# One buffer moved from the gate/up products to the w_down loads in a Mamba block with a ternary feed-forward

## The chip, the cores and the metric

The kernel runs on the 8 cores of one Trainium2 chip. The 4 x 4096 tokens are split into 8 runs of 2048 tokens, one for each core, and the cores do not exchange data. The time is that of the slowest core in device microseconds, from launch to end. Engines are called PE (TensorE, matrix products), DVE (VectorE), ACT (ScalarE), POOL (GpSimd) and SP (SyncE, which here only issues transfers).

## The reference

```python
xn = _layernorm(x, axis=-1)
x = x + _L0_attn_ref(xn, ...) + _L0_ffn_ref(xn, w_gate, w_up, w_down)

# _L0_attn_ref: a Mamba block (input projection, causal convolution, selective scan
# in chunks of 256 tokens, gating, output projection); the change does not touch it

def _weight_quant(w):                       # ternary weights, one scale for the matrix
    scale = 1.0 / jnp.clip(jnp.mean(jnp.abs(w)), 1e-05)
    return jnp.clip(jnp.round(w * scale), -1.0, 1.0) / scale
def _act_quant(x):                          # 8-bit activations, one scale for each token
    scale = 127.0 / jnp.clip(jnp.max(jnp.abs(x), axis=-1, keepdims=True), 1e-05)
    return jnp.clip(jnp.round(x * scale), -128.0, 127.0) / scale
def _bitlinear(x, w):
    return jnp.einsum('bsi,oi->bso', _act_quant(x), _weight_quant(w))
gate = silu(_bitlinear(x, w_gate))          # HIDDEN 1024 -> INNER 4096
up = _bitlinear(x, w_up)
return _bitlinear(gate * up, w_down)        # INNER 4096 -> HIDDEN 1024
```

## The kernel before

The program has four stages: normalization and weight casts, the Mamba block (which takes most of the time), the gate/up stage, and the down projection. A barrier stands between them. The change lies in the gate/up stage.

Every operation is recorded by a helper, `P.op`, with its queue (engine) and with the names (tags) of what it reads and writes. From the tags the helper derives the semaphore waits. An engine works through its list in the order in which the operations were recorded, and so does SP's queue: a transfer whose wait is not over holds all that were recorded behind it. Tags stand for buffers: a tile with two buffers has two tags, and a write to one of them waits only for the readers of that one.

The gate/up stage runs in eight passes, f = 0 to 7, of 512 of the 4096 inner columns each. For each pass:

- `f1_mm(f)` goes over the 16 tiles of 128 tokens (mt). For each it records 8 matmuls into a gate PSUM tile and 8 into an up PSUM tile (L939, 512 columns each; three such pairs of PSUM tiles take turns), then on ACT silu of the gate into `gsb` (L946) and the scaled up part into `usb` (L949), then on DVE the product of the two into `gu_bf` (L952) and its largest absolute value (L956). `gsb` and `usb` have two buffers each, by mt % 2.
- `f1_quant(f + 1)` makes the ternary weights of the next pass: 16 groups, 8 for gate and 8 for up, each a load of a 128 x 512 float32 tile on SP's queue into `wqf` (L916, two buffers) and two operations on DVE (L919 into `wts`, L923 into `wgq` or `wuq`). The weights of pass 0 are made before the passes start.
- `f1_wd` makes the ternary w_down for the next stage, in 64 pieces over all passes: a load of a 128 x 512 float32 tile on SP's queue into `wqf3` (L982, one buffer), two operations on DVE as one step (L986 into `wts`, L989 into `wdstg`, one buffer), and a store from `wdstg` to `s_wdq` on POOL's queue (L994).

`_sec(f)` mixes the last two: three steps of `f1_quant` (one whole group), then two steps of `f1_wd` (so that a load, a pair and a store fall on alternate places), and so on; at most 32 steps of `f1_wd` are taken in a pass, so that its 192 steps are used up in passes 0 to 5. `_zipf` records two steps of `f1_mm` for one step of `_sec`. The 48 + 32 steps of `_sec` thus lie beside the first 8 of the 16 token tiles of passes 0 to 5; the other 8 tiles have nothing beside them. Pass 6 has the 48 weight steps alone, and pass 7 nothing.

The trace names tiles by their allocation without the buffer's number, so that `wqf3` appears as `wqf` in it; its loads are told by their source, `wqf<-wdT`. The PSUM tiles appear as psB, psG (gate) and psC, psU (up).

Of the kernel before, what the change touches and what calls it, by code (L numbers as in the profile page):

```python
# [8 lines left out]
F32 = mybir.dt.float32  # L9
BF16 = mybir.dt.bfloat16  # L10
# [132 lines left out]
def build_program(TOK):  # L143
# [34 lines left out]
    def salloc(stack, name, shape, dt):  # L178
        return stack.enter_context(nc.sbuf_tensor(name, shape, dt))
# [5 lines left out]
    swbc = salloc(pstack, "swbc", [128, 9], F32)  # L185
# [60 lines left out]
         reads=["alraw"], writes=["alneg_t"])  # L246
    P.op("vector", lambda v: v.tensor_scalar_mul(alneg[:], alneg[:], -1.0),
         reads=["alneg_t"], writes=["alneg"])
# [4 lines left out]
        writes=["wcf:0"], dma=True)  # L253
    P.op("vector", lambda v: v.tensor_copy(wxT_bf[:], wcf[0][:, 0:16 * 96]),
         reads=["wcf:0"], writes=["wxT_bf"])
    P.op("sync", lambda e: e.dma_start(wcf[1][0:64, 0:DI], w_dtT.ap()),
         writes=["wcf:1"], dma=True)
    P.op("vector", lambda v: v.tensor_copy(wdtT_bf[:], wcf[1][0:64, 0:DI]),
         reads=["wcf:1"], writes=["wdtT_bf"])
# [569 lines left out]
    for sc in range(NSC):  # L829
# [7 lines left out]
        else:  # L837
# [11 lines left out]
         reads=["ones1"] + ["acc:%d:%d" % (wi2, t2) for wi2 in range(3)  # L849
                            for t2 in range(32)],  # L850
         writes=["psA"], wr_override=["psA"])
    P.op("scalar", lambda s: s.activation(acc[0:1, 0:96], psA[0:1, 0:96], AF.Copy,
                                          bias=0.0, scale=1.0),
         reads=["psA"], writes=["accr"])
    for wi in range(3):
        P.op("vector", lambda v, wi=wi: v.reduce_sum(
            swrow[0:1, 12 + wi:13 + wi], acc[0:1, wi * 32:(wi + 1) * 32], axis=AXX),
            reads=["accr"], writes=["swsum"])
    P.op("vector", lambda v: v.tensor_scalar(swrow[0:1, 0:3], swrow[0:1, 12:15],
                                             1.0 / NW_ELEMS, 1e-5, ALU.mult, ALU.max),  # L860
         reads=["swsum"], writes=["swclip"])
    P.op("vector", lambda v: v.tensor_scalar_mul(swrow[0:1, 3:6], swrow[0:1, 0:3], 0.5),
         reads=["swclip"], writes=["swthr"])
    P.op("vector", lambda v: v.tensor_scalar_mul(swrow[0:1, 6:9], swrow[0:1, 0:3], -0.5),
         reads=["swclip"], writes=["swnthr"])
    P.op("tensor", lambda t: t.matmul(psA[:, 0:9], ones2[0:1, 0:128], swrow[0:1, 0:9],
                                      start=True, stop=True),
         reads=["ones2", "swclip", "swthr", "swnthr"], writes=["psA"], wr_override=["psA"])
    P.op("vector", lambda v: v.tensor_copy(swbc[:], psA[:, 0:9]),
         reads=["psA"], writes=["swbc"])  # L870
# [6 lines left out]
    fstk = ExitStack()  # L877
# [3 lines left out]
    wqf = [salloc(fstk, "wqf%d" % i, [128, 512], F32) for i in range(2)]  # L881
    wts_1 = salloc(fstk, "wts", [128, 512], F32)
    wts = [wts_1, wts_1]
    gsb = [salloc(fstk, "gsb%d" % i, [128, 512], BF16) for i in range(2)]
    usb = [salloc(fstk, "usb%d" % i, [128, 512], BF16) for i in range(2)]
    wdstg = salloc(fstk, "wdstg", [128, 512], BF16)
    wqf3_1 = salloc(fstk, "wqf3", [128, 512], F32)
    wqf3 = [wqf3_1, wqf3_1]
    psG2 = fstk.enter_context(nc.psum_tensor("psG2", [128, 512], F32))
    psU2 = fstk.enter_context(nc.psum_tensor("psU2", [128, 512], F32))  # L890
    psG3 = fstk.enter_context(nc.psum_tensor("psG3", [128, 512], F32))
# [4 lines left out]
    for k2 in range(8):  # L896
        P.op("sync", lambda e, k2=k2: e.dma_start(
            xqfm[:, k2 * TOK:(k2 + 1) * TOK], s_xqfm.ap()[k2 * 128:(k2 + 1) * 128, :]),
            reads=["sxq:%d:%d" % (k2, i2) for i2 in range(NT)],
            writes=["xqfm:%d" % k2], dma=True)  # L900

    for i in range(NT):
        P.op("vector", lambda v, i=i: v.tensor_mul(
            combog[:, i:i + 1], invsx[:, i:i + 1], swbc[:, 0:1]),
            reads=["invsx:%d" % i, "swbc"], writes=["cg:%d" % i])
        P.op("vector", lambda v, i=i: v.tensor_mul(
            combou[:, i:i + 1], invsx[:, i:i + 1], swbc[:, 1:2]),
            reads=["invsx:%d" % i, "swbc"], writes=["cu:%d" % i])
# [20 lines left out]
    def f1_mm(f):  # L929
        fb = f % 2  # L930
        for mt in range(NT):
            gb = mt % 2
            psg, psgt = psGpool[mt % 3]
            psu, psut = psUpool[mt % 3]
            for (wtag, ps_, pst_) in (("wgq", psg, psgt), ("wuq", psu, psut)):
                wq_ = wgq[fb] if wtag == "wgq" else wuq[fb]
                for k2 in range(8):
                    yield lambda wq_=wq_, k2=k2, mt=mt, ps_=ps_, pst_=pst_, wtag=wtag, fb=fb: P.op(
                        "tensor", lambda t: t.matmul(  # L939
                            ps_[:, 0:512],  # L940
                            xqfm[:, k2 * TOK + mt * 128:k2 * TOK + (mt + 1) * 128],
                            wq_[:, k2 * 512:(k2 + 1) * 512], start=(k2 == 0), stop=(k2 == 7)),
                        reads=["xqfm:%d" % k2, "%s:%d:%d" % (wtag, fb, k2)],
                        writes=([pst_] if k2 == 0 else ()),
                        wr_override=([pst_] if k2 == 7 else ()))
            yield lambda gb=gb, mt=mt, psg=psg, psgt=psgt: P.op("scalar", lambda s: s.activation(  # L946
                gsb[gb][:], psg[:, 0:512], AF.Silu, bias=0.0, scale=combog[:, mt:mt + 1]),
                reads=[psgt, "cg:%d" % mt], writes=["gsb:%d" % gb])
            yield lambda gb=gb, mt=mt, psu=psu, psut=psut: P.op("scalar", lambda s: s.activation(  # L949
                usb[gb][:], psu[:, 0:512], AF.Copy, bias=0.0, scale=combou[:, mt:mt + 1]),  # L950
                reads=[psut, "cu:%d" % mt], writes=["usb:%d" % gb])
            yield lambda gb=gb, mt=mt, f=f: P.op("vector", lambda v: v.tensor_mul(  # L952
                gu_bf[:, mt * INNER + f * 512:mt * INNER + (f + 1) * 512],
                gsb[gb][:], usb[gb][:]),
                reads=["gsb:%d" % gb, "usb:%d" % gb], writes=["gu:%d:%d" % (mt, f)])
            yield lambda gb=gb, mt=mt, f=f: P.op("vector", lambda v: v.reduce_max(  # L956
                gmparts[:, mt * 8 + f:mt * 8 + f + 1],
                gu_bf[:, mt * INNER + f * 512:mt * INNER + (f + 1) * 512],
                axis=AXX, apply_absolute_value=True),
                reads=["gu:%d:%d" % (mt, f)], writes=["gmp:%d:%d" % (mt, f)])  # L960
# [17 lines left out]
    def f1_wd():  # L978
        for t in range(32):
            for hcol in range(2):  # L980
                wb9 = (t * 2 + hcol) % 2
                yield lambda t=t, hcol=hcol, wb9=wb9: P.op("sync", lambda e: e.dma_start(  # L982
                    wqf3[wb9][:], wdT.ap()[t * 128:(t + 1) * 128, hcol * 512:(hcol + 1) * 512]),
                    writes=["wqf3"], dma=True)
                def _wdq_pair(wb9=wb9):
                    P.op("vector", lambda v: v.tensor_single_scalar(  # L986
                        wts[0][:], wqf3[wb9][:], swbc[:, 8:9], ALU.is_le),
                        reads=["wqf3", "swbc"], writes=["wts"])
                    P.op("vector", lambda v: v.scalar_tensor_tensor(  # L989
                        wdstg[:], wqf3[wb9][:], swbc[:, 5:6], wts[0][:], ALU.is_ge,  # L990
                        ALU.subtract),
                        reads=["wqf3", "wts", "swbc"], writes=["wdstg"])
                yield _wdq_pair
                yield lambda t=t, hcol=hcol: P.op("gpsimd", lambda e: e.dma_start(  # L994
                    s_wdq.ap()[t * 128:(t + 1) * 128, hcol * 512:(hcol + 1) * 512],
                    wdstg[:]),
                    reads=["wdstg"], writes=["swdq:%d:%d" % (t, hcol)], dma=True)

    wd_it = iter(f1_wd())

    def _sec(f):
# [22 lines left out]
    for f in range(8):  # L1024
        _zipf(iter(f1_mm(f)), _sec(f), 2, 1)
# [3 lines left out]
    for mt in range(NT):  # L1029
        P.op("vector", lambda v, mt=mt: v.reduce_max(  # L1030
            sgu[:, mt:mt + 1], gmparts[:, mt * 8:mt * 8 + 8], axis=AXX),
            reads=["gmp:%d:%d" % (mt, f2) for f2 in range(8)], writes=["gmax:%d" % mt])
        P.op("vector", lambda v, mt=mt: v.tensor_single_scalar(
            invsgu[:, mt:mt + 1], sgu[:, mt:mt + 1], 1e-5, ALU.max),
            reads=["gmax:%d" % mt], writes=["gclip:%d" % mt])
        P.op("vector", lambda v, mt=mt: v.reciprocal(
            gmparts[:, mt * 8:mt * 8 + 1], invsgu[:, mt:mt + 1]),
            reads=["gclip:%d" % mt], writes=["grcp:%d" % mt])
        P.op("vector", lambda v, mt=mt: v.tensor_scalar_mul(
            sgu[:, mt:mt + 1], gmparts[:, mt * 8:mt * 8 + 1], 127.0),  # L1040
            reads=["grcp:%d" % mt], writes=["sgu:%d" % mt])
        P.op("vector", lambda v, mt=mt: v.tensor_scalar_mul(
            invsgu[:, mt:mt + 1], invsgu[:, mt:mt + 1], 1.0 / 127.0),
            reads=["gclip:%d" % mt], writes=["invsgu:%d" % mt])
        P.op("vector", lambda v, mt=mt: v.tensor_mul(
            combod[:, mt:mt + 1], invsgu[:, mt:mt + 1], swbc[:, 2:3]),
            reads=["invsgu:%d" % mt, "swbc"], writes=["cd:%d" % mt])
# [129 lines left out]
def _get_nc(TOK):  # L1177
    if TOK not in _NC_CACHE:
        _NC_CACHE[TOK] = build_program(TOK)
    return _NC_CACHE[TOK]  # L1180
# [62 lines left out]
```

How the kernel before makes its waits and increments, by code:

```python
                def body(eng, lst=lst, q=q):  # L119
                    sat = {}
                    last_inc = {}
                    for o in lst:
                        wl = {}
                        for d in o.waits:
                            if d.cum > wl.get(d.skey, 0):
                                wl[d.skey] = d.cum
                        for k in sorted(wl, key=lambda t: (t[0], t[1])):
                            v = wl[k]
                            if v > sat.get(k, 0):
                                eng.wait_ge(sems[k], v)
                                sat[k] = v
                        inst = o.fn(eng) if o.fn is not None else None
                        if o.inc:
                            k = o.skey
                            amt = o.cum - last_inc.get(k, 0)
                            inst.then_inc(sems[k], amt)
                            last_inc[k] = o.cum
```

## Time and profile before

| what | value |
|---|---|
| time, median of 2 runs | 5199.21 us (5197.51 to 5200.91) |
| time of the profiled execution | 5203.91 us |
| its span on the slowest core (core 0) | 5202.3 us (other cores 5163.9 to 5197.3) |
| busy: DVE, ACT, PE, POOL | 73%, 36%, 31%, 3% of the span |
| gate/up stage, first load issued to last product | about 4110 to 4748 us |

The profile shows one execution on the slowest core. An engine counts as busy while it executes; PE's share is that of pipelined matmuls and says little on how near it is to its peak. A line such as "L952" is that line of the kernel. In the waits a pair "A <- B" means that A stood idle until B was done. The stage that the change touches is one eighth of the span, and so the shares of the whole span say little about it; it is read by stretches.

### The profile page before, as it was taken

How to read it: one execution, taken by the hardware profiler on the slowest of the kernel's cores; microseconds unless marked ns; L12 is line 12 of the kernel's file. 1: busy time of each engine (PE TensorE's matmuls, PEld its weight loads, DVE VectorE, ACT ScalarE, POOL GpSimd, SP SyncE). 2: the span in 40 equal slices, each digit the busy share in tenths (PEclk: the TensorE clock that was granted, in tenths of full speed). 3: DMA queues.
4: the chain of work that ended last, by engine and by line, in shares of the span. 5: the costliest groups of instructions: out<-in, count | busy, mean ns of one | idle time of the engine just before them, and what ended most of it. 6: DMA issues, size and time to landing. Idle time of an engine off the chain costs nothing.

```text
span 5202.3 us, 47037 instructions; the slowest of 8 cores (5163.9 to 5202.3 us)
## 1 busy us (share of the span) xinstructions
PE 1622.3 (31%) x7308; PEld 818.5 (16%) x7308; DVE 3800.4 (73%) x10735; ACT 1858.8 (36%) x4106; POOL 151.6 (3%) x252
## 2 busy tenths in 40 slices
PE   0134111410321051033105103310200278776776
PEld 0122000200210030012002001200000033333332
DVE  3436888888888888888888888888888566653232
ACT  1335344434443434344333432433223022223342
POOL 0200000000000000000000000000000000000000
PEclk9996555755655575565557555655555689898998
DMA  7542002401410240041004002100100333321665
GB/s 239 170 116 69 0 21 72 122 0 47 135 33 0 89 126 0 25 129 53 0 0 118 1 0 61 57 0 0 49 0 0 110 118 102 101 90 37 205 219 190
DMA packets 311056, 378.41 MB, mean 73 GB/s; under 512 B 15522, under 2 KB 253218, under 8 KB 308644
## 3 DMA queue, kind: packets, MB, share of 16 engines
q1 hardware_dynamic: 282532, 266.34, 17.0%
q0 software_dynamic: 26496, 96.48, 5.3%
q10 hardware_dynamic: 1728, 12.58, 0.8%
q14 instruction: 234, 1.92, 0.1%
q8 instruction: 66, 1.08, 0.1%
HBM read 329.22 MB, written 46.14 MB: 72 GB/s over the span
## 4 chain that ended last, share of the span: by engine, by line
DVE 38%; issue 19%; PE 16%; DMA 14%; ACT 11%; DVEq 1%; SPq 0%; ACTq 0%; POOL 0%; POOLq 0%
DVE hbuf L677 12%; DVE dbub L670 6%; DVE ypb L699 4%; ACT dAb L661 4%; DVE ypb L695 3%; DMA wdqt<-s_wdq 3%; PE psBC L640 2%; PE psI L510 2%; PE psP L1119 2%; DVE yA L702 2%; PE psBC L647 2%; DMA wo_buf<-s_woutT 2%; DMA wch<-s_winT 2%; DVE pa L691 2%; DMA s_wdq<-wdstg 2%
## 5 line engine op out<-in xcount | busy, mean ns | idle before, releaser
L677 DVE TENSOR_TENSOR_SCAN hbuf<-dAb,dbub 128x256 bf16<-128x256 bf16 x2048 | 1398.5, 683 | 189.7 <-ACT dAb L661 189.4
L661 ACT ACTIVATE dAb<-delta_t,alneg 128x256 bf16<-128x256 bf16 x2048 | 906.0, 500 | 74.7 <-DVE hbuf L677 65.1
L640 PE MATMUL psBC<-shstB,ones 1*128 1x256 f32 x256 | 146.0, 669 | 2013.8 <-DVE shstB L637 2013.8
L651 ACT ACTIVATE Bsb<-psBC 128x256 bf16<-128x256 f32 x128 | 49.1, 383 | 1885.1 <-PE psBC L647 1845.0
L670 DVE TENSOR_TENSOR dbub<-du_t,Bsb 128x256 bf16<-128x256 bf16 x2048 | 579.6, 283 | 5.9 <-ACT Bsb L651 2.4
L702 DVE TENSOR_TENSOR yA<-yA,ypb 128x256 f32<-128x256 f32 x1024 | 435.1, 425 | 109.5 <-DVE ypb L699 4.5
L640 PEld LDWEIGHTS psBC<-shstB,ones 1*128 1x128 f32 x256 | 61.2, 295 | 2068.3 <-issue 2068.3
L699 DVE TENSOR_TENSOR ypb<-ypb,pa 128x256 bf16<-128x256 bf16 x896 | 261.7, 292 | 95.5 <-DVE ypb L695 3.2
L510 PE MATMUL psI<-xnsc,wch 128*128 128x256 bf16 x2048 | 307.2, 314 | 72.8 <-DMA wch<-s_winT 59.2
L752 PE MATMUL psOut<-wo_buf,gated 128*128 128x512 bf16 x256 | 118.5, 463 | 498.6 <-DVE gated L724 432.2
L695 DVE TENSOR_TENSOR ypb<-hbuf,Csb 128x256 bf16<-128x256 bf16 x1024 | 273.2, 267 | 0.0
L510 PEld LDWEIGHTS psI<-xnsc,wch 128*128 128x128 bf16 x2048 | 218.0, 112 | 166.5 <-issue 117.2
L691 DVE TENSOR_TENSOR pa<-hbuf,Csb 128x256 bf16<-128x256 bf16 x896 | 235.9, 263 | 0.0
L939 PE MATMUL psG<-wgq,xqfm 128*128 128x512 bf16 x640 | 171.3, 416 | 72.3 <-ACT gsb L946 71.9
L1119 PE MATMUL psP<-wdqt,guqT 128*128 128x512 bf16 x640 | 172.4, 409 | 46.1 <-DMA wdqt<-s_wdq 46.1
L939 PE MATMUL psU<-wuq,xqfm 128*128 128x512 bf16 x640 | 157.6, 391 | 0.0
L1079 DVE TENSOR_SCALAR tqg<-tqg 128x1024 int32<-128x1024 int32 x64 | 44.2, 691 | 149.7 <-ACT tqg L1073 149.2
L946 ACT ACTIVATE gsb<-psG,combog 128x512 bf16<-128x512 f32 x80 | 55.0, 688 | 226.5 <-DVE gu_bf L952 182.3
L1097 ACT ACTIVATE guqT<-psTf 128x1024 bf16<-128x1024 bf16 x64 | 65.4, 1022 | 186.1 <-PE psTf L1090 186.1
L919 DVE TENSOR_SCALAR wts<-wqf,swbc 128x512 f32<-128x512 f32 x128 | 62.0, 484 | 95.5 <-DMA wqf<-wuT 47.3
L647 PE MATMUL psBC<-shstC,ones 1*128 1x256 f32 x256 | 130.0, 607 | 0.0
L601 PE MATMUL psB<-dltbf,wdtT_bf 64*128 64x256 bf16 x128 | 48.0, 375 | 251.7 <-ACT xpb L605 231.5
(156 smaller groups left out, 3371.1 us busy)
## 6 DMA issues: line engine op xcount, KB each, us to landing
wch<-s_winT SPq DMA_DIRECT2D x128, 512.0 KB, 5.3
wdqt<-s_wdq SPq DMA_DIRECT2D x64, 1024.0 KB, 6.5
wo_buf<-s_woutT SPq DMA_DIRECT2D x64, 512.0 KB, 4.9
wab<-wgT POOLq DMA_DIRECT2D x32, 512.0 KB, 3.8
wab<-wuT POOLq DMA_DIRECT2D x32, 512.0 KB, 3.6
wab<-wdT POOLq DMA_DIRECT2D x32, 512.0 KB, 3.5
wqf<-wgT SPq DMA_DIRECT2D x64, 256.0 KB, 3.4
wqf<-wuT SPq DMA_DIRECT2D x64, 256.0 KB, 3.4
```

Of the source, the lines that this page charges most:

```text
L510: "tensor", lambda t: t.matmul(psI[mp][:, 0:CH], wch[wb][:, k2 * 256 + m * 128:k2 * 256 + (m + 1) * 128], xnsc[p][:, k2 * CH:(k2 + 1) * CH ...
L640: P.op("tensor", lambda t, bk=bk: t.matmul(psBC[bk][:, 0:CH], ones2[64:65, 0:128], shstB[64:65, :], start=True, stop=True), reads=["shB", ...
L647: P.op("tensor", lambda t, bk=bk: t.matmul(psBC[bk][:, CH:2 * CH], ones2[64:65, 0:128], shstC[64:65, :], start=True, stop=True), reads=["s ...
L661: P.op("scalar", lambda s, q=q, n=n, b=b: s.activation(dAb[b][:], delta_t[p][:, q * CH:(q + 1) * CH], AF.Exp, bias=0.0, scale=alneg[:, q * ...
L670: P.op("vector", lambda v, q=q, b3=b3, e2=e2: v.tensor_mul(dbub[b3][:], du_t[p][:, q * CH:(q + 1) * CH], Bsb[e2][:]), reads=["du:%d:%d" % ...
L677: P.op("vector", lambda v, b=b, b3=b3: v.tensor_tensor_scan(hbuf[b3][:], dAb[b][:], dbub[b3][:], 0.0, ALU.mult, ALU.add), reads=["dA:%d" % ...
L691: P.op("vector", lambda v, q=q, b3=b3, e2=e2: v.tensor_mul(pa[q][:], hbuf[b3][:], Csb[e2][:]), reads=["h:%d" % b3, "Csb:%d" % e2], writes= ...
L695: P.op("vector", lambda v, q=q, b=b, b3=b3, e2=e2: v.tensor_mul(ypb[b][:], hbuf[b3][:], Csb[e2][:]), reads=["h:%d" % b3, "Csb:%d" % e2], w ...
L699: P.op("vector", lambda v, q=q, b=b: v.tensor_add(ypb[b][:], ypb[b][:], pa[q][:]), reads=["yp:%d" % b, "pa:%d" % q], writes=["yp:%d" % b])
L702: P.op("vector", lambda v, q=q, b=b: v.tensor_add(yA[:, q * CH:(q + 1) * CH], yA[:, q * CH:(q + 1) * CH], ypb[b][:]), reads=["yA:%d" % q, ...
L939: "tensor", lambda t: t.matmul(ps_[:, 0:512], xqfm[:, k2 * TOK + mt * 128:k2 * TOK + (mt + 1) * 128], wq_[:, k2 * 512:(k2 + 1) * 512], sta ...
L1119: "tensor", lambda t: t.matmul(psP[pp][j][:, 0:512], guqT[gb][j][:, kb * 128:(kb + 1) * 128], wdqt[wb3][:, k3 * 512:(k3 + 1) * 512], start ...
```

## The change

`gsb` and `usb` go from two buffers each to one (128 x 512 bf16), and `wqf3` goes from one buffer to two (128 x 512 float32). The bytes that come free are those that are taken. The tags follow: one tag for `gsb`, one for `usb`, two for `wqf3`. No operation is added, removed or reordered.

```diff
-    gsb = [salloc(fstk, "gsb%d" % i, [128, 512], BF16) for i in range(2)]
-    usb = [salloc(fstk, "usb%d" % i, [128, 512], BF16) for i in range(2)]
+    gsb_1 = salloc(fstk, "gsb", [128, 512], BF16)
+    usb_1 = salloc(fstk, "usb", [128, 512], BF16)
+    gsb = [gsb_1, gsb_1]
+    usb = [usb_1, usb_1]
     wdstg = salloc(fstk, "wdstg", [128, 512], BF16)
-    wqf3_1 = salloc(fstk, "wqf3", [128, 512], F32)
-    wqf3 = [wqf3_1, wqf3_1]
+    wqf3 = [salloc(fstk, "wqf3_%d" % i, [128, 512], F32) for i in range(2)]
...
                 gsb[gb][:], psg[:, 0:512], AF.Silu, bias=0.0, scale=combog[:, mt:mt + 1]),
-                reads=[psgt, "cg:%d" % mt], writes=["gsb:%d" % gb])
+                reads=[psgt, "cg:%d" % mt], writes=["gsb"])
...
                 usb[gb][:], psu[:, 0:512], AF.Copy, bias=0.0, scale=combou[:, mt:mt + 1]),
-                reads=[psut, "cu:%d" % mt], writes=["usb:%d" % gb])
+                reads=[psut, "cu:%d" % mt], writes=["usb"])
...
                 gsb[gb][:], usb[gb][:]),
-                reads=["gsb:%d" % gb, "usb:%d" % gb], writes=["gu:%d:%d" % (mt, f)])
+                reads=["gsb", "usb"], writes=["gu:%d:%d" % (mt, f)])
...
                     wqf3[wb9][:], wdT.ap()[t * 128:(t + 1) * 128, hcol * 512:(hcol + 1) * 512]),
-                    writes=["wqf3"], dma=True)
+                    writes=["wqf3:%d" % wb9], dma=True)
...
-                        reads=["wqf3", "swbc"], writes=["wts"])
+                        reads=["wqf3:%d" % wb9, "swbc"], writes=["wts"])
...
-                        reads=["wqf3", "wts", "swbc"], writes=["wdstg"])
+                        reads=["wqf3:%d" % wb9, "wts", "swbc"], writes=["wdstg"])
```

## Rows read from the trace of the kernel before

**Rows 1.** Busy time by stretch (start:end length, engines, clock, DMA): first mixed half.

```profile
4154.58:4217.15 62.57, 45.99 (x181) 18.66 (x180) 41.40 (x71) 11.86 (x19) 5.41 (x10) 0.85 0.39 131
```

**Rows 2.** Waits, 4110 to 4760 us: who waited for whom: us, times, longest.

```profile
ACT gsb L946 <- DVE gu_bf L952: 288.8, 47, 9.7
...
DVE wts L919 <- DMA wqf<-wuT: 47.3, 30, 3.3
DVE wts L919 <- DMA wqf<-wgT: 42.8, 25, 7.0
...
DVE wts L986 <- DMA wqf<-wdT: 22.1, 30, 1.4
...
DVE wdstg L989 <- DMA s_wdq<-wdstg: 19.7, 29, 1.4
```

**Rows 3.** The 64 stores of L994: from issue to landing.

```profile
DMA to landing us min/median/max: 2.0/3.7/4.4
```

**Rows 4.** Timeline, two intervals: start us, us, engine, line, operation [idle before].

```profile
4163.78 0.75 DVE L989 SCALAR_TENSOR_TENSOR wdstg<-wqf,swbc,wts 128x512 bf16<-128x512 f32 x1
...
4165.07 0.55 POOL L994 DMA_DIRECT2D s_wdq<-wdstg  x1 [6.61 <-DVE wdstg L989]
...
4165.90 0.42 DVE L952 TENSOR_TENSOR gu_bf<-gsb,usb 128x512 bf16<-128x512 bf16 x1
...
4166.42 0.69 DVE L956 TENSOR_REDUCE gmparts<-gu_bf 128x1 f32<-128x512 bf16 x1
...
4167.31 0.49 DVE L986 TENSOR_SCALAR wts<-wqf,swbc 128x512 f32<-128x512 f32 x1 [0.20 <-DMA wqf<-wdT]
4168.59 0.75 DVE L989 SCALAR_TENSOR_TENSOR wdstg<-wqf,swbc,wts 128x512 bf16<-128x512 f32 x1 [0.80 <-DMA s_wdq<-wdstg]
4169.43 0.33 SPq L982 DMA_DIRECT2D wqf<-wdT  x1
...
4169.85 1.35 SPq L916 DMA_DIRECT2D wqf<-wgT  x2
...
4173.06 0.49 DVE L919 TENSOR_SCALAR wts<-wqf,swbc 128x512 f32<-128x512 f32 x1 [2.27 <-DMA wqf<-wgT]
...
4174.51 0.49 DVE L986 TENSOR_SCALAR wts<-wqf,swbc 128x512 f32<-128x512 f32 x1
4175.10 0.75 DVE L989 SCALAR_TENSOR_TENSOR wdstg<-wqf,swbc,wts 128x512 bf16<-128x512 f32 x1
```

**Rows 5.** L989 in passes 0 to 5: count, duration in ns, first and last start.

```profile
L989 DVE SCALAR_TENSOR_TENSOR wdstg<-wqf,swbc,wts x11: 750/752/752, 4156.6 to 4216.4; 128x512 bf16<-128x512 f32 x11
L989 DVE SCALAR_TENSOR_TENSOR wdstg<-wqf,swbc,wts x10: 750/752/752, 4235.6 to 4288.9; 128x512 bf16<-128x512 f32 x10
L989 DVE SCALAR_TENSOR_TENSOR wdstg<-wqf,swbc,wts x11: 750/752/752, 4310.5 to 4369.7; 128x512 bf16<-128x512 f32 x11
L989 DVE SCALAR_TENSOR_TENSOR wdstg<-wqf,swbc,wts x11: 750/751/752, 4391.2 to 4453.3; 128x512 bf16<-128x512 f32 x11
L989 DVE SCALAR_TENSOR_TENSOR wdstg<-wqf,swbc,wts x10: 750/751/752, 4473.2 to 4527.2; 128x512 bf16<-128x512 f32 x10
L989 DVE SCALAR_TENSOR_TENSOR wdstg<-wqf,swbc,wts x11: 750/752/753, 4548.8 to 4609.0; 128x512 bf16<-128x512 f32 x11
```

**Rows 6.** Timeline: PE's release at the first light half, then its pace there.

```profile
4213.89 0.69 ACT L946 ACTIVATE gsb<-psB,combog 128x512 bf16<-128x512 f32 x1 [5.50 <-DVE gu_bf L952]
...
4214.82 0.58 PE L939 MATMUL psB<-wgq,xqfm 128*128 128x512 bf16 x1 [3.15 <-ACT gsb L946]
...
4226.78 0.69 ACT L949 ACTIVATE usb<-psU,combou 128x512 bf16<-128x512 f32 x1 [0.98 <-PE psU L939]
4227.57 0.42 DVE L952 TENSOR_TENSOR gu_bf<-gsb,usb 128x512 bf16<-128x512 bf16 x1 [2.24 <-ACT usb L949]
...
4228.57 0.69 ACT L946 ACTIVATE gsb<-psB,combog 128x512 bf16<-128x512 f32 x1 [1.09 <-PE psB L939]
...
4231.03 0.42 DVE L952 TENSOR_TENSOR gu_bf<-gsb,usb 128x512 bf16<-128x512 bf16 x1 [2.24 <-ACT usb L949]
```

## The prediction

> **What bounds the kernel now.** I read the page first: the span is 5202.3 us, VectorE (DVE) is the busiest engine at 73%, and its 40 slices show that the end of the program is a different stage from the long scan. The change touches only tiles of the gate/up stage, so I looked for that stage's start and end by its lines (about 4110 to 4760 us) and then asked the trace for the waits in it, for single stretches of its timeline, and for the stretches it is made of.
>
> The stage is eight passes (f = 0 to 7). In passes 0 to 5 the first half is a *mixed half*: DVE quantizes the next pass's gate and up weights and, in between, w_down pieces. In the first mixed half PE is busy 46 of 62.6 us and DVE 41 [rows 1]: neither is full, so waits set the time. The waits of the whole stage name them [rows 2]: DVE waits 47.3 + 42.8 us for `wqf` loads, 22.1 us for `wqf3` loads (the trace calls them wqf<-wdT) and 19.7 us for the store that must leave `wdstg` before it is written again. ScalarE (ACT) waits 288.8 us for the product on DVE to free `gsb`. In the second half (the *light half*) DVE has only products and maxima to do and TensorE (PE) sets the pace.
>
> The unit to read is the interval from one w_down quantization (L989) to the next. By the order in which work is emitted there are two kinds: *short* ones with one weight group (L919 and L923) between two L989, and *long* ones with two. In passes 0 to 5 there are 58 intervals, 30 short and 28 long; 14 of the long ones also hold a product and its maximum. First to last L989 of the six passes adds up to 59.8 + 53.3 + 59.2 + 62.1 + 54.0 + 60.2 = 348.6 us [rows 5].
>
> A short one [rows 4]: L989 starts at 4163.78 and ends at 4164.53, POOL issues the store at 4165.07, and the next L989 starts at 4168.59 after a wait for that store. A long one follows: it ends at 4169.34, only then is the next `wqf3` load issued (4169.43), and queued behind it on SP's queue is a `wqf` load (4169.85). DVE stands for 2.27 us until that lands (4173.06), and L989 starts at 4175.10. The interval is 6.51 us.
>
> **wqf3, one buffer to two.** No instruction is added; 64 loads wait for the quantization two back instead of the last. In long intervals the removed wait is the one that sets the end: SP's queue is held by the `wqf3` load, not by the `wqf` buffer, so the second weight group's load can now leave as soon as the group two before it is done. That is before the previous L989 ends, one short interval earlier. With a load time of 3.2 us (4169.85 to 4173.06 [rows 4]) it has landed when DVE comes to it. What is late next? Two candidates:
>
> - the `wdstg` store, which the change leaves single: 0.54 us to its issue (4164.53 to 4165.07 [rows 4]), 3.7 us to landing (the median [rows 3]), 0.12 us to the next L989 (4165.07 + 3.4 landed, 4168.59 started), 0.75 us of L989: 5.11 us;
> - DVE's own work: a weight group costs 1.45 us (4173.06 to 4174.51 [rows 4]), the w_down pair, of the same two shapes, 1.45, product and maximum 1.2 (4165.90 to 4166.42 + 0.69). A long interval with a product is 3 x 1.45 + 1.2 = 5.55, without one 4.35, a short one 2 x 1.45 + 1.2 = 4.1 at most.
>
> So 30 short and 14 long intervals are set by the store at 5.11, and 14 by DVE at 5.55: 44 x 5.11 + 14 x 5.55 = 302.5. In short intervals the `wqf3` wait merely becomes a longer wait for the store. Saved: 348.6 - 302.5 = 46.1 us. Bounds: landings go from 2.0 to 4.4 us [rows 3]; I take the median because stores will still fly beside loads as now. Passes 6 and 7 hold no w_down work and save nothing.
>
> The Trainium skill (DMA: Bandwidth & Descriptors, Anatomy of one DMA) prices such a POOL-issued transfer at about 2.0 us plus its bytes over 436 GB/s, which for 128 KB is an estimated 2.3 us; by it the store would not bind at all and the sum would be that of the fast store below. The trace's 3.7 us median disagrees with it.
>
> **gsb and usb, two buffers to one.** Instructions and durations stay. `gsb` of token tile mt+1 now waits for the product of mt, not of mt-1. In the mixed half two products are some 5 us or more apart and gsb plus usb need 1.4, so DVE never waits for this. In the light half PE sets 3.46 us per tile (4227.57 to 4231.03 [rows 6]); usb ends at 4227.47, the product at 4227.99, and the next gsb starts at 4228.57 because PE's psB ends then. The new wait ends 0.5 us before the old one, so the pace stays. If that cover were gone it would cost at most its excess, tile by tile.
>
> What is lost is lead. In the mixed half PE runs until PSUM's three pairs and the two `gsb` are full, then stands: at 4214.82 it starts a tile after 3.15 us of standing, released by the gsb that the product just freed (4213.89 [rows 6]). With one buffer less, that same release lets it start the tile *before*: one more tile of 3.46 us is still to do in the light half, which ends with PE. This happens in every pass with a mixed half and in pass 6, whose first part has weight groups alone: 7 x 3.46 = 24.2 us more. Pass 7 is PE from end to end and adds none. Bounds: 0, if PE gets the tile done while DVE works off the other four, and 48 if each such tile ran at the lower of PE's two clock levels, 1.2 instead of 2.4 GHz, where it takes twice as long (the granted clock of 0.85 in [rows 1] shows both levels in a mixed half); 24.2 is nearest to the rows, since PE was standing at the release.
>
> **Sum.** 46.1 - 24.2 = 21.9 us less. The profiled execution (span 5202.3, time 5203.9) would become 5182; it lies 4.7 us above the median of the runs shown, 5199.2, so the forecast is 5199.2 - 21.9 = **5177 us**.
>
> **Rivals.**
>
> *Slow store (slower).* One mechanism: the `wqf3` and `wqf` loads leave earlier and lie over the store, which then lands later. At the longest landing seen, 4.4 us, the store interval is 0.54 + 4.4 + 0.12 + 0.75 = 5.81, above DVE's 5.55, so all 58 take it: 337.0, saved 11.6, lost 24.2: +12.6, **5212 us**. It decides from 348.6 - 58 x g = 24.2, g = 5.59, a landing of 4.18 us. For it: landings vary from 2.0 to 4.4 already. Against: today's stores leave in the same half microsecond as two loads [rows 4], and still take 3.7. The Trainium skill (SBUF — State Buffer, SBUF: two separate sides) says that DVE in some modes keeps POOL from writing descriptors, which speaks against packing DVE denser. The trace does not show it: at 4165.07 POOL issues on its usual 0.54 us while DVE has work.
>
> *Fast store.* With the loads spread out, stores land in 2.0 us (the shortest landing [rows 3]); then DVE alone sets the mixed half: 30 x 4.1 + 14 x 4.35 + 14 x 5.55 = 261.6, saved 87.0, less 24.2: **5136 us**. Against: many loads stay in flight.
>
> *The lost buffer is free.* PE fills its lead otherwise, and only the 46.1 counts: **5153 us**. Against: PE's stand at the release.
>
> *The change doesn't do what it says.* The long wait is written down to `wqf` loads, not `wqf3` [rows 2]; if `wqf`'s own buffers held them, long intervals would stay and only the 24.2 is left: **5223 us**. Against: SP issues that load 0.42 us behind the `wqf3` load [rows 4], while the group that frees its buffer was done before L989 began.
>
> **How the numbers follow.** Forecast 0.62 (its own range, landings of 3.4 to 4.0 us: store intervals 4.81 and 5.41, sums 289.3 and 315.7, so 5164 to 5191), slow store 0.14, lost buffer free 0.10, fast store 0.08, no effect on long intervals 0.06. The range from 5150 to 5210 holds the forecast, the free buffer and about half of the slow store; the two outer cases and the rest of the slow store stay out. Two per cent, about what a measurement of this kernel can tell from no change, is 104 us; no case lies further than 63 from the median. Hence 0.98 for within 2%, and 0.01 for each side for what I have not thought of.
>
> **What would show it.** Right: L986's waits for wqf<-wdT near 0; L919's waits for `wqf` down from 90 to about 30 us (the pass-0 weights ahead of the passes, and pass 6, keep theirs); L989's waits for the store up from 19.7 to some 40 to 50; L989 first to last some 50 us per pass with long and short intervals nearly equal; in each light half PE busy for one tile more, some 3.5 us; ACT's wait for the product as large as before or larger. Wrong: landings of s_wdq far from 3.7 us (then fast or slow store decides); long intervals still near 6.5 us with the wait on `wqf`; DVE's product waiting for usb inside mixed halves, or tiles more than 3.5 us apart in pass 7, which would mean that the single `gsb` binds where I cost it at nothing; a changed time in any other stage.

## The result, and the profile after

The changed kernel takes 5152.9 us (median of 7 runs, 5143.2 to 5157.6) where the kernel before takes 5200.4 beside it (6 runs, 5190.2 to 5204.2): a ratio of 0.991, with an interval of 0.9898 to 0.9923, 47.5 us less. Run again beside the experiments it took 5155.3 us, a ratio of 0.9891 [0.9876, 0.9906] to 5211.5. The forecast was 22 us less: the direction and the range held, the size was less than half of what was measured.

All line numbers of the changed kernel are one higher than before (L986 is L987, L989 is L990, L994 is L995, and so on). The profiled execution took 5160.9 us. First the page's line on the span, then the waits of the gate/up stage (4106 to 4712 us: who waited for whom, us, times, longest), which answer to [rows 2]:

```profile
span 5159.3 us, 47069 instructions; the slowest of 8 cores (5115.3 to 5159.3 us)
```

```profile
ACT gsb L947 <- DVE gu_bf L953: 231.1, 61, 6.9
...
DVE wdstg L990 <- DMA s_wdq<-wdstg: 27.3, 30, 1.9
DVE wts L920 <- DMA wqf<-wgT: 26.5, 18, 7.2
...
DVE wts L920 <- DMA wqf<-wuT: 15.0, 13, 2.3
```

DVE's waits for `wqf` fall from 90.1 to 41.5 us, the wait of L987 for a `wqf3` load (22.1 us before) is gone from the list, and the wait for the store grows only from 19.7 to 27.3, in 30 instances, one in each short interval and none in a long one. The w_down quantizations pass by pass (count, duration in ns, first and last start) answer to [rows 5]:

```profile
L990 DVE SCALAR_TENSOR_TENSOR wdstg<-wqf,swbc,wts x11: 751/752/752, 4153.6 to 4202.3; 128x512 bf16<-128x512 f32 x11
L990 DVE SCALAR_TENSOR_TENSOR wdstg<-wqf,swbc,wts x10: 750/752/752, 4224.1 to 4267.0; 128x512 bf16<-128x512 f32 x10
L990 DVE SCALAR_TENSOR_TENSOR wdstg<-wqf,swbc,wts x11: 751/752/752, 4292.1 to 4339.5; 128x512 bf16<-128x512 f32 x11
L990 DVE SCALAR_TENSOR_TENSOR wdstg<-wqf,swbc,wts x11: 750/752/752, 4365.6 to 4414.3; 128x512 bf16<-128x512 f32 x11
L990 DVE SCALAR_TENSOR_TENSOR wdstg<-wqf,swbc,wts x10: 750/752/752, 4436.0 to 4480.0; 128x512 bf16<-128x512 f32 x10
L990 DVE SCALAR_TENSOR_TENSOR wdstg<-wqf,swbc,wts x11: 750/752/753, 4505.2 to 4552.5; 128x512 bf16<-128x512 f32 x11
```

First to last, the six passes add up to 279.1 us (from starts with two decimals: 48.76 + 42.98 + 47.43 + 48.69 + 43.93 + 47.28), where before it was 348.6. That is 69.5 us saved, not 46.1. From the start of each L990 to the next, by the kinds of the prediction (each short interval holds a product too):

| interval | count | before, mean us | forecast | after, mean us |
|---|---|---|---|---|
| short | 30 | 5.13 | 5.11 | 4.79 |
| long without a product | 14 | 6.89 | 5.11 | 4.39 |
| long with a product | 14 | 7.03 | 5.55 | 5.27 |

The timeline of DVE (start us, us, engine, line, operation, [idle before]) shows one short interval and one long one:

```profile
4158.85 0.75 DVE L990 SCALAR_TENSOR_TENSOR wdstg<-wqf,swbc,wts 128x512 bf16<-128x512 f32 x1
4160.59 0.49 DVE L920 TENSOR_SCALAR wts<-wqf,swbc 128x512 f32<-128x512 f32 x1 [1.00 <-DMA wqf<-wgT]
...
4162.98 0.48 DVE L987 TENSOR_SCALAR wts<-wqf,swbc 128x512 f32<-128x512 f32 x1
4164.22 0.75 DVE L990 SCALAR_TENSOR_TENSOR wdstg<-wqf,swbc,wts 128x512 bf16<-128x512 f32 x1 [0.76 <-DMA s_wdq<-wdstg]
4165.08 0.49 DVE L920 TENSOR_SCALAR wts<-wqf,swbc 128x512 f32<-128x512 f32 x1
...
4166.53 0.49 DVE L920 TENSOR_SCALAR wts<-wqf,swbc 128x512 f32<-128x512 f32 x1
...
4167.98 0.49 DVE L987 TENSOR_SCALAR wts<-wqf,swbc 128x512 f32<-128x512 f32 x1
4168.57 0.75 DVE L990 SCALAR_TENSOR_TENSOR wdstg<-wqf,swbc,wts 128x512 bf16<-128x512 f32 x1
```

The short interval (4158.85 to 4164.22) ends with a wait for the store; with 1.00 us of waiting for a `wqf` load in it as well, it is longer than the mean of 4.79. The long one (4164.22 to 4168.57, 4.35 us) has no wait in it at all: DVE's own two weight groups and the pair fill it. By the prediction it should have waited for the store until 5.11.

Why it does not, SP's and POOL's timelines around the two stores show (L917 and L983 are the loads of `wqf` and `wqf3`), and below them the time from issue to landing of the first store, of the second, and of all 64, which answers to [rows 3]:

```profile
4158.23 0.33 SPq L917 DMA_DIRECT2D wqf<-wgT  x1
4159.68 0.33 SPq L983 DMA_DIRECT2D wqf<-wdT  x1
...
4166.51 0.33 SPq L917 DMA_DIRECT2D wqf<-wgT  x1
4166.93 0.38 SPq L983 DMA_DIRECT2D wqf<-wdT  x1
```

```profile
4160.13 0.55 POOL L995 DMA_DIRECT2D s_wdq<-wdstg  x1 [4.73 <-DVE wdstg L990]
4165.51 0.54 POOL L995 DMA_DIRECT2D s_wdq<-wdstg  x1 [4.83 <-DVE wdstg L990]
```

```profile
DMA to landing us min/median/max: 3.9/3.9/3.9
...
DMA to landing us min/median/max: 2.0/2.0/2.0
...
DMA to landing us min/median/max: 2.0/2.4/4.6
```

The first store is issued 0.45 us behind a `wqf3` load (and 1.90 us behind a `wqf` load) and lands in 3.9 us. The second has a `wqf` load 1.00 us and its `wqf3` load 1.42 us *behind* it and lands in 2.0: loads that leave behind a store did not hold it up. This repeats: through the first mixed half the stores that begin short intervals land in 3.0 to 3.9 us, each with a `wqf3` load 0.45 us ahead, and those that begin long ones in 2.0 or 2.1. Before the change every store of that stretch had a `wqf3` load 0.45 us and a `wqf` load some 0.03 us ahead, and landed in 3.3 to 4.1.

In the trace before, one store of pass 2 had the `wqf3` load alone just ahead of it; the `wqf` load left 0.30 us behind. It landed in 3.1 us, as stores with one load ahead do after the change (SP's timeline, POOL's, and the landing of this store):

```profile
4335.08 0.33 SPq L982 DMA_DIRECT2D wqf<-wdT  x1
4335.83 0.33 SPq L916 DMA_DIRECT2D wqf<-wuT  x1
...
4335.53 0.54 POOL L994 DMA_DIRECT2D s_wdq<-wdstg  x1 [6.34 <-DVE wdstg L989]
...
DMA to landing us min/median/max: 3.1/3.1/3.1
```

The traces of all eight cores say the same of the stores that begin an interval. Before, 456 with both loads just ahead landed in 3.75 us in the median, and 8 with the `wqf3` load alone in 3.23. After, 240 with one load 0.4 to 0.8 us ahead landed in 3.27, and 224 with no load in the 1.8 us ahead of them in 2.00.

The other part of the change came out as forecast. From the eighth product of a pass (the last in the mixed half) to the sixteenth, the light halves of passes 0 to 5 grow from 105.2 us in sum to 123.0, and pass 6 from 56.1 to 60.9 (first to last product): 22.6 us in all, forecast 24.2. The start of the first light half, on DVE, beside [rows 6]:

```profile
4204.87 0.42 DVE L953 TENSOR_TENSOR gu_bf<-gsb,usb 128x512 bf16<-128x512 bf16 x1 [0.67 <-ACT usb L950]
...
4206.76 0.42 DVE L953 TENSOR_TENSOR gu_bf<-gsb,usb 128x512 bf16<-128x512 bf16 x1 [0.67 <-ACT usb L950]
...
4215.99 0.42 DVE L953 TENSOR_TENSOR gu_bf<-gsb,usb 128x512 bf16<-128x512 bf16 x1 [2.24 <-ACT usb L950]
...
4219.45 0.42 DVE L953 TENSOR_TENSOR gu_bf<-gsb,usb 128x512 bf16<-128x512 bf16 x1 [2.24 <-ACT usb L950]
```

At first PE's lead is worked off, 1.89 us per tile: with one `gsb` and one `usb`, silu, scaled copy and product of a tile follow each other before the next tile's silu starts. When the lead is gone, tiles are 3.46 us apart, PE's pace. First to last product, the stage takes 542.0 us instead of 587.5: 45.5 less, and that is the change (69.5 saved, 22.6 lost, the rest in the steps between the halves).

### The profile page after: what moved, and what is told of

It is laid out like the page before. It is cut to its first block, busy times and chain, and to the rows that moved or that the text cites. A ratio compares the mean times of both kernels' runs of the same rounds, so it can differ in the third digit from the quotient of the medians.

```text
span 5159.3 us, 47069 instructions; the slowest of 8 cores (5115.3 to 5159.3 us)
## 1 busy us (share of the span) xinstructions
PE 1622.7 (31%) x7308; PEld 816.3 (16%) x7308; DVE 3800.4 (74%) x10735; ACT 1858.9 (36%) x4106; POOL 151.0 (3%) x252
## 4 chain that ended last, share of the span: by engine, by line
DVE 38%; issue 20%; PE 16%; DMA 13%; ACT 11%; DVEq 1%; ACTq 0%; SPq 0%; POOL 0%; POOLq 0%
DVE hbuf L677 12%; DVE dbub L670 6%; DVE ypb L699 4%; ACT dAb L661 4%; DVE ypb L695 3%; DMA wdqt<-s_wdq 3%; PE psBC L640 2%; PE psP L1120 2%; DMA wch<-s_winT 2%; DVE yA L702 2%; PE psBC L647 2%; PE psG L940 2%; DVE pa L691 2%; PE psU L940 1%; PE psI L510 1%
## 5 line engine op out<-in xcount | busy, mean ns | idle before, releaser
L640 PEld LDWEIGHTS psBC<-shstB,ones 1*128 1x128 f32 x256 | 60.9, 294 | 2074.2 <-issue 2074.2
L1120 PE MATMUL psP<-wdqt,guqT 128*128 128x512 bf16 x640 | 183.7, 428 | 36.3 <-DMA wdqt<-s_wdq 35.9
L953 DVE TENSOR_TENSOR gu_bf<-gsb,usb 128x512 bf16<-128x512 bf16 x128 | 54.0, 422 | 112.8 <-ACT usb L950 112.8
```

The costliest lines, as they stand in the source:

```text
L640: P.op("tensor", lambda t, bk=bk: t.matmul(psBC[bk][:, 0:CH], ones2[64:65, 0:128], shstB[64:65, :], start=True, stop=True), reads=["shB", ...
L1120: "tensor", lambda t: t.matmul(psP[pp][j][:, 0:512], guqT[gb][j][:, kb * 128:(kb + 1) * 128], wdqt[wb3][:, k3 * 512:(k3 + 1) * 512], start ...
```

## The experiments

Theory A: the store's landing is set by the loads issued just ahead of it. The second `wqf3` buffer moves half of those loads behind their store, so that only 30 of 58 intervals still wait for it; the lost `gsb` and `usb` cost one PE tile in each light half and in pass 6. Rival B: the single `gsb` and `usb` cost nothing, and the `wqf3` part is worth the measured 47 us alone. Rival C: the store's landing does not depend on what the load ahead of it moves.

**The wqf3 part alone.** Two buffers for `wqf3`; `gsb` and `usb` keep two as well. Room for the second ones comes from places of `gu_bf` that are first written in pass 7.

```diff
+    gsb = [salloc(fstk, "gsb", ...), gu_bf[:, 14 * INNER + 7 * 512:14 * INNER + 8 * 512]]
+    usb = [salloc(fstk, "usb", ...), gu_bf[:, 15 * INNER + 7 * 512:15 * INNER + 8 * 512]]
...
+    wqf3 = [salloc(fstk, "wqf3_%d" % i, [128, 512], F32) for i in range(2)]
...
+            gb = mt % 2 if f < 7 else 0
```

> wqf3 has two buffers as in the changed kernel, and gsb and usb keep two as before (their second buffers are parts of gu_bf that are written only in pass 7, where one buffer is used). Theory A (the wqf3 part is worth 69 us, the lost gsb/usb buffer costs 24): first to last L989-type step in passes 0 to 5 sums to about 279 us as in the changed kernel, light halves as in the kernel before, time about 5200 - 69 = 5131 us. Rival B (the wqf3 part is worth 46 us as predicted, and the lost buffer is free): no faster than the changed kernel, about 5153 us.

Measured: 5138.5 us, ratio 0.9866 [0.9853, 0.9878] to 5210.9, so 72 us less by the medians and 70 by the ratio. The intervals add up to 279.1 us, as in the changed kernel (short 4.80, long 4.36 and 5.28), and the light halves stay at what they were before (16.3 to 17.9 us from the eighth product to the last). The waits for the store here:

```profile
DVE wdstg L988 <- DMA s_wdq<-wdstg: 31.8, 30, 2.0
```

Again 30 waits, one for each short interval. The wqf3 part is worth some 70 us, not 46.

**The gsb and usb part alone.** `wqf3` keeps one buffer.

```diff
-    gsb = [salloc(fstk, "gsb%d" % i, [128, 512], BF16) for i in range(2)]
-    usb = [salloc(fstk, "usb%d" % i, [128, 512], BF16) for i in range(2)]
...
+    gsb = [gsb_1, gsb_1]
+    usb = [usb_1, usb_1]
```

> gsb and usb have one buffer, wqf3 keeps its one. Theory A: about 24 us slower than the kernel before, 5224 us; intervals between w_down quantizations stay at 5.1 and 7.0 us, and every light half is longer by one PE tile of 3.46 us. Rival B (the lost buffer is free): 5200 us, light halves unchanged. Stores land in 3.3 to 4.1 us by both, as two loads still leave with each.

Measured: 5232.9 us, ratio 1.0051 [1.0034, 1.0068], so 22 us more by the medians and 27 by the ratio. The intervals hardly move (351.1 us in sum); the light halves of passes 0 to 5 grow by 19.1 us (124.3 against 105.2) and pass 6 by 4.6. Rival B falls: the lost buffer costs what the prediction said. The landings of the store stay as before, since the loads leave as before:

```profile
DMA to landing us min/median/max: 2.0/3.8/4.5
```

The two parts add up: by the medians 72 less and 22 more make 50 less (43 by the ratios), beside the 47.5 and 56 of the two measurements of the whole change.

**The store taken out.** The changed kernel with a second `wdstg`, so that no quantization waits for a store.

```diff
+    wdstg = [salloc(fstk, "wdstg", ...), gu_bf[:, 13 * INNER + 7 * 512:13 * INNER + 8 * 512]]
...
-                        wdstg[:], wqf3[wb9][:], ...
+                        wdstg[wb9][:, 0:512], wqf3[wb9][:], ...
```

> The changed kernel with a second wdstg buffer (a part of gu_bf that is written only in pass 7). If the store is what sets the short intervals of the changed kernel (mean 4.79 us), they fall to DVE's own work of about 4.0 us: 30 x 0.79 = 24 us less, about 5129 us, and no wait for s_wdq is left. If loads set them as well, they stay at 4.5 us or more and the time falls by less than 10 us.

Measured: 5136.5 us, ratio 0.9859 [0.9845, 0.9873]. Short intervals fall to 3.84 us, long ones grow slightly (4.52 and 5.45, 4.3 us in sum), and the total is 254.9, 24.2 less than in the changed kernel. No wait for a store is left. So the store held the short intervals alone, by 28.5 us in sum, and the long ones were DVE's own work already.

**Smaller loads ahead of the store.** The changed kernel; the w_down loads bring 128 of their 512 columns, the rest of `wqf3` is zero. The w_down product is thus that of a quarter of the weights, and the kernel leaves out the rest.

```diff
-                    wqf3[wb9][:], wdT.ap()[t * 128:(t + 1) * 128, hcol * 512:(hcol + 1) * 512]),
+                    wqf3[wb9][:, 0:128], wdT.ap()[t * 128:(t + 1) * 128, hcol * 512:hcol * 512 + 128]),
```

> The changed kernel with w_down loads of 128 of the 512 columns (64 KB instead of 256 KB); the rest of wqf3 is set to zero once, so that w_down's weights are not those of the reference. Theory A (a store lands late because a load was issued half a microsecond ahead of it): the stores of short intervals, 3.0 to 3.9 us now, land in 2.0 to 2.5 us, short intervals fall from 4.79 to about 4.1 us, time about 5133 us. Rival C (a store's landing depends on what DVE and POOL do then, not on the loads): landings of 3.0 to 3.9 us in short intervals stay, and so does the time, 5153 us.

Measured: 5136.7 us, ratio 0.9861 [0.9848, 0.9874]. Order and buffers are those of the changed kernel, and the store is what it was; only the load ahead is a quarter. Landings of all stores, and the waits for them:

```profile
DMA to landing us min/median/max: 2.0/2.1/3.2
```

```profile
DVE wdstg L990 <- DMA s_wdq<-wdstg: 4.9, 12, 0.8
```

In the first mixed half the stores with a load 0.45 us ahead of them now land in 2.0 to 2.7 us, not 3.0 to 3.9. The wait falls from 27.3 to 4.9 us, and short intervals to 3.98 us. Rival C falls and theory A stands: how much the load just ahead moves decides when the store lands. The `wqf` load some 1.9 us ahead of the same stores was of full size in this run too, so it is not what made them late. A quarter of the bytes here also means rows a quarter as long, and no run tells the two apart.

**More lead, wqf3 left single.** From the kernel before: silu is written straight into its place in `gu_bf` and the product is made there, so that `gsb` is not needed, and `usb` has five buffers (four in `gu_bf`).

```diff
+    usb = [salloc(fstk, "usb", ...)] + [gu_bf[:, m9 * INNER + 7 * 512:m9 * INNER + 8 * 512] for m9 in (12, 13, 14, 15)]
...
+            gb = mt % NUB if f < 7 else 0
...
-                gsb[gb][:], psg[:, 0:512], AF.Silu, ...
+                gu_bf[:, mt * INNER + f * 512:mt * INNER + (f + 1) * 512], psg[:, 0:512], AF.Silu, ...
```

> The kernel before with its single wqf3, no gsb (silu goes into its place in gu_bf) and five usb: three tiles more lead than before. Theory A (each tile of lead is worth 3.46 us in each of seven passes): mixed halves stay at 348 us in all, light halves shorten by 10.4 us each, 7 x 10.4 = 73 us less, about 0.986 of the kernel before. Rival B (lead is free): no change.

Measured: 5154.2 us, ratio 0.9901 [0.9885, 0.9916], so 57 us less by the medians and 52 by the ratio; the expected 73 were missed. The timeline of DVE in a light half shows where the rule "3.46 us for each tile of lead" ends:

```profile
4294.60 0.41 DVE L953 TENSOR_TENSOR gu_bf<-gu_bf 128x512 bf16<-128x512 bf16 x1
4295.12 0.69 DVE L958 TENSOR_REDUCE gmparts<-gu_bf 128x1 f32<-128x512 bf16 x1
4295.72 0.41 DVE L953 TENSOR_TENSOR gu_bf<-gu_bf 128x512 bf16<-128x512 bf16 x1
```

Products come 1.12 us apart, product and maximum without a gap: PE's lead now covers the light half, and DVE sets it. Eight tiles at 1.12 are 9.0 us, and three of the six light halves stand at 8.97. In sum they go from 105.2 to 59.4, which is 45.8 less instead of 6 x 3 x 3.46 = 62.3; pass 6 gives another 11.0. On this core the mixed halves give 8 us back: their intervals add up to 356.5 instead of 348.6, with landings of 3.9 us in the median instead of 3.7. 45.8 + 11.0 - 7.9 = 48.9 agrees with the stage, which is 48.6 us shorter from first to last product. The 8 us are no more than the spread of the cores: these sums range from 348.6 to 354.3 over the eight cores before and from 349.6 to 359.2 here, 351.5 and 354.0 in the mean. That stores land later here is thus not shown; over the eight cores the stage is 54.8 us shorter in the mean.

**All together.** Two `wqf3`, two `wdstg`, silu in place and five `usb`, in no more bytes than the kernel before, with the places in `gu_bf` that are free until pass 7.

```diff
+    usb = [usb_1] + [gu_bf[:, m9 * INNER + 7 * 512:m9 * INNER + 8 * 512] for m9 in (12, 13, 14, 15)]
+    wdstg = [salloc(fstk, "wdstg", ...), gu_bf[:, 11 * INNER + 7 * 512:11 * INNER + 8 * 512]]
+    wqf3 = [salloc(fstk, "wqf3_%d" % i, [128, 512], F32) for i in range(2)]
```

> Two wqf3, two wdstg, no gsb at all (ACT writes silu of the gate into its place in gu_bf and the product is taken in place) and five usb (one own, four parts of gu_bf that are written only in pass 7). By theory A mixed halves fall to DVE's work (about 255 us in six passes, as in e3_wdstg_two) and PE, four tiles further ahead than in the changed kernel, never stands in passes 0 to 6: a pass is 16 x 3.46 = 55 us, the stage about 8 x 55 + 10 = 450 us from first to last product against 542, time about 5065 us. If lead beyond one more tile brings nothing (PE held by something else), it is no faster than e3_wdstg_two, 0.986 of the kernel before, about 5130 us.

Measured: 5057.2 us, ratio 0.9704 [0.9691, 0.9718], 154 us less than before and faster than the changed kernel by some 98. The intervals add up to 254.9, as with two `wdstg` above, the light halves to 56.7, and pass 6 to 45.1: 93.7 + 48.5 + 11.0 = 153.2 saved. The stage itself, from first to last product, is 151.2 us shorter. The three savings, each with its own buffer, add up: the store and the `wqf3` load ended different intervals of the mixed halves, and the lead shortens the light ones.

**The changed kernel again**, beside these two, gave the second measurement above.

> The changed kernel beside the others on one chip: 0.991 of the kernel before.

## Why the prediction was wrong

**Which wait ends the long intervals: right.** It was the `wqf3` load in front of the `wqf` load on SP's queue, and not `wqf`'s own buffers. With two `wqf3` the waits for `wqf` fall to 41.5 us (forecast about 30) and those of L987 to nothing, and the wqf3 part alone shows it without the other edit. "The change doesn't do what it says" is out.

**What is late next: wrong for the 14 long intervals without a product, too dear for the others.** The step that failed is the store's term in the sum, "I take the median because stores will still fly beside loads as now", 3.7 us. It was one value for the 44 intervals that the prediction gave to the store, where after the change there are two kinds of stores. Stores that begin a short interval still have a load 0.45 us ahead, but one where there were two, and land in 3.0 to 3.9 us in the first mixed half (3.2 in the median of all 30). Stores that begin a long one have none just ahead and land in 2.0 to 2.1. The long ones without a product therefore end with DVE's own work, 4.39 (forecast 5.11; DVE's own work was priced at 4.35, rightly), and save 14 x 0.72 = 10.1 us more than forecast; the short ones, at 4.79, 30 x 0.32 = 9.5 more. The long ones with a product were DVE's, as forecast, but at 5.27 and not 5.55, and save 14 x 0.28 = 3.9 more: product and maximum add 0.9 us to such an interval and not 1.2, since DVE starts an operation before the record of the last one ends (the timeline of the run with more lead has 0.60 us from the start of a maximum to the next product, 4295.12 to 4295.72, and the maximum itself at 0.69). Together that is 23.5 us, but for rounding the gap between 46.1 and 69.5.

The rows for it were there. The prediction had read that a `wqf3` load leaves as soon as L989 ends, 0.45 us ahead of the store, and that a `wqf` load is queued behind it on SP. After the change the order on SP's queue decides: in long intervals the `wqf3` load stands behind a `wqf` load that waits for a weight group *inside* the interval (in the example it leaves at 4166.93, after the first of that interval's two groups, which ends at 4166.42; the `wqf` load leaves at 4166.51), and so it cannot leave ahead of the store. Working through SP's queue once for a short and once for a long interval would have put half of the stores at the shortest landing and half at the median: 30 x 5.11 + 14 x 4.35 + 14 x 5.55 = 291.9, so 56.7 saved and 5167 us, nearer but still 14 us too high.

**The rivals.** "Slow store" named the same mechanism, loads beside stores, with the wrong sign: the loads that moved now leave well ahead of a store (the `wqf` load of a short interval 1.90 us, before 0.03) or behind it, and neither holds it up. "Fast store" had the right sign for the long intervals alone: taken for all of them it gave 5136. The result lies between it and the forecast. The Trainium skill (DMA: Bandwidth & Descriptors, Anatomy of one DMA) prices each such store at an estimated 2.3 us. The trace after comes near that for stores with no load just ahead, 2.0, and disagrees for those with one, 3.0 to 3.9; the median of all 64, 2.4, only lies between the two kinds. "The lost buffer is free" gave 5153, which is the time that was measured, but by luck: the lost buffer cost 22.6 us and the wqf3 part saved 69.5, not 46.1, and the two errors nearly cancel.

**The lost buffer: right.** One PE tile per light half and in pass 6: 24.2 forecast, 22.6 in the trace of the changed kernel, 23.8 in the trace of the buffer alone, whose time rose by 22 to 27. Pass 7 stays at 3.46 us per tile, and no product waits for `usb` in mixed halves, as forecast. What was not foreseen is that the light half's first tiles are 1.89 us apart (ACT and DVE in turn on one buffer); it costs nothing, because PE ends the light half.

**The signs.** ACT's wait for the product was to be as large or larger; it fell from 288.8 to 231.1 us. The lost buffer alone did raise it, to 317.2, but the shorter mixed halves lower it more: with the wqf3 part alone it is 211.2 (108.1 + 103.1, for the two buffers of `gsb`). Store waits of 40 to 50 us were forecast and 27.3 came; 50 us per pass, and 43.0 to 48.8 came.

**The sum.** 5199.2 - 69.5 + 22.6 = 5152.3, against 5152.9 measured. That it comes so close is partly luck, since 69.5 and 22.6 are read on one core of one execution each. In the mean of the eight cores the intervals fall from 351.5 to 279.8 us, light halves and pass 6 grow from 162.3 to 183.2, and the stage is 50.4 us shorter, beside the 47.5 and 56 of the two measurements. With the store's two landings and the smaller price of the product in it, the rest of the working stands.

## What to carry to other kernels

Here the same store took from 2.0 to 3.9 us, by what was issued just ahead of it. Before a median of landings is carried over, work out for each kind of interval which transfers will stand ahead of it on the queues after the change. A second buffer that lets a load leave earlier also changes what other transfers it flies beside: of the 69.5 us saved here the prediction missed 19.6 for that reason. Lead in tiles (PSUM pairs plus the buffers behind them) can be priced at the slower engine's time per tile, but only until the faster engine's own work fills the stretch: here three more tiles of lead gave 7.6 us per light half and not 10.4.

## What the runs showed of the hardware

In the first mixed half a 128 KB store issued by POOL landed in 2.0 or 2.1 us when the last load had left 1.9 us or more ahead of it, though two more left 1.0 and 1.4 us behind it. It landed in 3.0 to 3.9 with one 256 KB load 0.45 us ahead, in 3.3 to 4.1 with two (0.45 and 0.03 us ahead, in the kernel before), and in 2.0 to 2.7 with a load of a quarter of those bytes 0.45 us ahead. Single stores elsewhere took longer: 2.7 us without a load just ahead, and 4.6 with one.

In the run with the quarter loads the light halves of passes 2 to 4 on the slowest core ran at a granted clock of 0.81, which is neither of the two levels of TensorE's clock. The stretch (start:end length; busy time of PE, PE's weight loads, DVE, ACT, POOL; clock; DMA share; GB/s), and below it the same for a light half of the changed kernel:

```profile
4405.00:4420.00 15.00, 15.00 (x59) 6.23 (x58) 5.51 (x11) 6.57 (x10) 0.00 (x0) 0.81 0.01 2
```

```profile
4205.00:4221.00 16.00, 16.00 (x76) 7.25 (x75) 7.98 (x15) 8.48 (x13) 0.00 (x0) 1.00 0.01 2
```

PE is busy without a gap in both, and a tile took 4.20 us at 0.81 instead of 3.46. The Trainium skill (TensorE: Matmul & The Clock Gate, Part 1: The HAM clock gate) names a current limit that takes a die to 13/16 of the clock, 0.81, when several of its cores run dense products. The row agrees with the level. It does not show a whole die: in the same stretch, counted from each core's own start, core 4 stands at 0.81 too, and cores 6 and 7 of that die at 1.00. Cores 4 and 5 hold 0.81 for 160 us on end (4340 to 4499 us); cores 6 and 7 hold it nowhere in their spans for more than 55. In the profile of the changed kernel it is again two neighbours: from 5025 to 5049 us, in the down projection, cores 2 and 3 stand at 0.81 and cores 0 and 1 of their die at 1.00. What brought it on was not tried.
